# A two-layer graph network on one core: other places for the adjacency's windows, the last tiles' normalisation, and TensorE's branch

## The reference, cut to what matters

```python
# layer 0 (500 hidden features)
h    = sigmoid(h0 @ wenc.T + benc)           # "encoder"
h2   = h @ conv_weight
agg  = segment_sum(h2[src] * edge_weight[:, None], dst)
x    = x + (agg + h @ lin_weight.T) @ wdec.T + bdec
# layer 1
h    = h1 @ W.T + b
deg  = 1 + number of edges with this src
msg  = deg[row]**-0.5 * deg[col]**-0.5 * h[col]     # self loops added
x    = x + segment_sum(msg, row)
```

## Time and profile before

| | us |
|---|---|
| median of 3 runs | 455.64 |
| lowest, highest | 454.35, 456.87 |
| the profiled execution's own time | 455.52 |
| its span | 453.7 |
| TensorE busy in the span | 444.1 |

### The profile page before, as it was taken

How to read it: one execution, slowest core, us unless ns; L and a number is a source line. 1 busy time by engine, 2 the same in 40 slices (tenths; PEclk the granted TensorE clock), 3 DMA queues, 4 the chain that set the end, 5 groups by cost and what they waited for, 6 DMA issues and landing times.

```text
span 453.7 us, 8837 instructions
## 1 busy us (share of the span) xinstructions
PE 444.1 (98%) x3202; PEld 332.8 (73%) x3202; DVE 301.2 (66%) x604; ACT 237.4 (52%) x452; POOL 41.3 (9%) x63
## 2 busy tenths in 40 slices
PE   6999998999999999999999999999999999999997
PEld 4999988978775465469888878888889844444454
DVE  5999895976864243864767776938471657567652
ACT  6987996657769552234244444658463622222220
POOL 2611200000000000000000000464600000000000
PEclk9999999999999999999999999999999999999999
DMA  7950958299457899045800006151758004323433
GB/s 288 306 175 2 173 87 145 70 317 317 143 162 138 265 79 325 3 124 186 302 13 1 1 0 228 53 186 46 287 213 293 1 7 167 129 92 140 156 119 111
DMA packets 48399, 66.37 MB, mean 146 GB/s; under 512 B 25793, under 2 KB 35024, under 8 KB 46820
## 3 DMA queue, kind: packets, MB, share of 16 engines
q1 hardware_dynamic: 48036, 65.39, 48.5%
q0 software_dynamic: 320, 0.39, 0.4%
HBM read 43.62 MB, written 16.77 MB: 133 GB/s over the span
## 4 chain that ended last, share of the span: by engine, by line
PE 84%; ACT 4%; DVE 4%; DMA 4%; SPq 2%; issue 1%; ACTq 0%; DVEq 0%
PE bank L1587 21%; PE bank L1588 21%; PE bank L1589 20%; PE bank L1603 19%; DMA benc_c<-benc 3%; PE bank L1712 2%; DMA h16T<-x 1%; SPq L696 1%; PE bank L1714 1%; ACT h0T L1027 1%; ACT stage L1076 1%; ACT h L979 1%; ACT cnt L1073 1%; DVE stats L1190 1%; DVE h0T L1310 1%
## 5 line engine op out<-in xcount | busy, mean ns | idle before, releaser
L1603 PE MATMUL bank<-a,h_hi 128*128 128x256 f16 (+3 forms) x400 | 85.5, 270 | 0.0
L1603 PE MATMUL bank<-a,h_lo 128*128 128x256 f16 (+3 forms) x400 | 85.5, 270 | 0.0
L1587 PE MATMUL bank<-right,left 128*128 128x512 f16 (+1 forms) x148 | 54.4, 367 | 0.0
L1588 PE MATMUL bank<-right,left 128*128 128x512 f16 (+1 forms) x148 | 54.4, 367 | 0.0
L1589 PE MATMUL bank<-right,left 128*128 128x512 f16 (+1 forms) x148 | 54.4, 367 | 0.0
L1152 ACT CAST left<-zs 128x512 f16<-128x512 f32 x35 | 21.5, 617 | 60.3 <-PE bank L1589 60.3
L1572 DVE SCALAR_TENSOR_TENSOR x<-bank,dis_u,x 128x512 f32<-128x512 f32 (+2 forms) x37 | 26.7, 722 | 34.2 <-PE bank L1589 34.2
L1587 PE MATMUL bank<-h0T,we 128*128 128x256 f32 (+3 forms) x144 | 41.4, 287 | 1.0 <-DVE h0T L1308 1.0
L1603 PEld LDWEIGHTS bank<-a,h_hi 128*128 128x128 f16 (+1 forms) x400 | 38.9, 97 | 4.2 <-issue 0.3
L1603 PEld LDWEIGHTS bank<-a,h_lo 128*128 128x128 f16 (+1 forms) x400 | 39.1, 98 | 3.8
L1587 PE MATMUL bank<-unit,g 128*128 128x500 f16 (+3 forms) x120 | 40.8, 340 | 0.0
(11 more groups left out here) (191 smaller groups left out, 978.2 us busy)
## 6 DMA issues: line engine op xcount, KB each, us to landing
whole<-w SPq DMA_DIRECT2D x7, 1024.0 KB, 7.8
adj_scratch<-stage SPq DMA_DIRECT2D x50, 125.0 KB, 3.5
right_scratch<-right SPq DMA_DIRECT2D x5, 1024.0 KB, 4.0
right<-right_scratch SPq DMA_DIRECT2D x5, 1024.0 KB, 4.8
h<-x SPq DMA_DIRECT2D x9, 512.0 KB, 6.7
x<-x SPq DMA_DIRECT2D x9, 512.0 KB, 5.4
out<-x SPq DMA_DIRECT2D x18, 256.0 KB
w_tile<-w SPq DMA_DIRECT2D x8, 512.0 KB, 4.9
```

Source lines behind the costliest of these rows:

```text
L1587: pe.matmul(o, lhs[0], rhs[0], start=first, stop=False, skip_group_check=True)
L1588: pe.matmul(o, lhs[0], rhs[1], start=False, stop=False, skip_group_check=True)
L1603: ins = pe.matmul(o, h1[i][0:n, k, 128 * f:128 * (f + 1)], moving, start=(k == 0 and part == 0 and i == 0), stop=(k == T - 1 and part == p ...
```

## The change

1. `due` is bent: 22 windows instead of 26 are due beside the encoder. Behind the groups from `("e", 1, 3)` there are now two or one, and 23 windows (0 to 22) stand ahead of `("g", 0)`. Behind `("g", 3)`, `("g", 5)` and `("g", 8)` stand three windows (29 to 31, 34 to 36, 41 to 43), and behind the other `g` and `swl` groups two.
2. ACT's normalisation of tiles 6 to 9 is two steps, `high` (L977) and `norm` (the f32 pass), with other work between them. The abs-sum of the conv weights (`("size", "wc")`, L993) moves from behind `("e", 2, 1)` to behind `("e", 1, 1)`. The turns of tiles 8 and 9 now stand together behind `("e", 2, 3)`; the cuts of the conv weights move from beside block 4 into blocks 3 and 4.
3. The maximum over partitions for the scales goes by one small matmul (`("spread", "wc")`) that broadcasts the 128 sums through the identity into a PSUM bank, and DVE reads that, instead of two DMAs through DRAM. It takes a turn in the rotation of six banks.
4. TensorE's program is written twice behind one test of the flag; the test ahead of layer 1 is gone.
5. The 2 KB load of `benc` is issued behind the second tile of x instead of behind the sixth. One abs-sum and load of `w1` moves from beside `swl` into layer 0's second stage, `bounds` two steps later.

```diff
+SLOW = 22
...
     beside = {
-        (1, 0): turn(2)[:2] + fourth[1:3] + turn(2)[2:], (1, 1): fourth[3:], (1, 2): [("norm", 6)] + fifth[:1], (1, 3): [("norm", 7), ("split", 6), ("turn", 6)],
-        (2, 0): [("split", 7), ("turn", 7)] + fifth[1:], (2, 1): [("size", "wc")], (2, 2): both(turn(3)) + [("norm", 8)],
-        (2, 3): [("norm", 9), ("split", 8), ("turn", 8), ("limits", "out")],
-        (3, 0): [("split", 9), ("turn", 9)], (3, 1): [("limits", "in")], (3, 2): both(turn(4)),
-        (4, 0): [("limits", "scale")], (4, 1): cut_wc[:1], (4, 2): cut_wc[1:3], (4, 3): cut_wc[3:],
+        (1, 0): turn(2)[:2] + fourth[1:3] + turn(2)[2:], (1, 1): fourth[3:] + [("size", "wc")], (1, 2): [("high", 6)] + fifth[:1], (1, 3): [("norm", 6), ("split", 6), ("turn", 6), ("high", 7)],
+        (2, 0): [("norm", 7), ("split", 7), ("turn", 7)] + fifth[1:], (2, 1): [("high", 8)], (2, 2): [("norm", 8)] + both(turn(3)) + [("high", 9)],
+        (2, 3): [("split", 8), ("turn", 8), ("norm", 9), ("split", 9), ("turn", 9), ("spread", "wc")],
+        (3, 0): [("limits", "scale")], (3, 1): cut_wc[:1], (3, 2): both(turn(4)), (3, 3): cut_wc[1:2],
+        (4, 0): cut_wc[2:3], (4, 1): cut_wc[3:],
     }
...
     def due(w):
-        return w + OPEN * (NW - w) / NW
+        if w < SLOW:
+            return OPEN + (share - OPEN) * w / SLOW
+        return share + (NW - share) * (w - SLOW) / (NW - SLOW)
+
+    groups = [s[0] for s in dense[dense.index(("edges",)):] if s[0] in ("e", "g", "swl")]
+    share = NW * groups.count("e") / len(groups)
...
-                elif s == ("limits", "out"):
-                    sp.wait_ge(sizes_ready, 1)
-                    sp.dma_start(limit_row, sizes[:]).then_inc(limits_out, 16)
...
+                elif s[0] == "high":
+                    t = s[1]
+                    n = tile_rows(t)
+                    act.wait_ge(rstd_ready, t // 2 + 1)
+                    if t >= 2 * BY_DMA + 2:
+                        act.wait_ge(turned[t - 2], 32)
...
+                    if s == ("spread", "wc"):
+                        pe.wait_ge(sizes_ready, 1)
+                        pe.matmul(take(s)[:, 0:P], sizes[:].broadcast_to([P, P]), ident[:], start=True, stop=True,
+                                  skip_group_check=True).then_inc(acc_ready, 1)
...
+            m = pe.value_load(missed[0:1, 0:1], min_val=0, max_val=1)
+            with pe.If(m == 0):
+                run(STEPS[general + 1:], (0,))
+            with pe.If(m != 0):
```

More of the change, by code:

```diff
@@ L192, in schedule @@
     dense += [("load", "wl")] + [("g", t) for t in range(4)] + mix(cut_wl, [("g", t) for t in range(4, T)]) + opening[:2]
-    for k, s in enumerate([("g", 2), ("g", 4), ("g", 6), ("g", 8), opening[0]]):
+    for k, s in enumerate([("g", 2), ("g", 4), ("g", 6), ("g", 8)]):
         i = dense.index(s) + 1
@@ L253, in schedule @@
                 steps += [("row", "in"), ("load", "wd")]
-            if n == 1 and k in (1, 2, 3):
-                steps += [("size", "w1", KD - 4 + k)] + [("load", "w1", KD - 2 + k)] * (k == 1)
+            if n == 1 and k in (1, 2, 3, 4):
+                steps += [("size", "w1", KD - 5 + k)] + [("load", "w1", KD - 3 + k)] * (k < 3)
             if n and sums and (n, k) != (1, 0):
@@ L358, in build @@
             frees[s[1:]] = len(frees)
+        elif s == ("limits", "scale"):
+            frees["spread", "wc"] = len(frees)
     nth = {(p, b): p * NB + b for p in range(NP) for b in range(NB)}
@@ L419, in build @@
         minus_half = small("minus_half", [P, 2], F32)
-        sizes = small("sizes", [P, 2], F32)
+        sizes = small("sizes", [P, 1], F32)
         ew_sizes = small("ew_sizes", [EP, 1], F32)
@@ L605, in build @@
         relu_ready = sem("relu_ready")
+        high_ready = sem("high_ready")
         split_ready = sem("split_ready")
@@ L698, in _ @@
                     sp.dma_start(ew_raw[:], nat_w).then_inc(ew_in, 16)
+                    sp.dma_start(benc_c[:], benc).then_inc(benc_in, 16)
                 if t == 3:
@@ L991, in _ @@
                     loaded(act, "wc", 0)
-                    act.wait_ge(size_blank, 1)
-                    nc.scalar.activation(wc_abs[:], wc_raw[:], ACT.Abs, accum_out=sizes[:, 0:1]).then_inc(sizes_ready, 1)
+                    nc.scalar.activation(wc_abs[:], wc_raw[:], ACT.Abs, accum_out=sizes[:]).then_inc(sizes_ready, 1)
                 elif s[0] == "degree":
@@ new lines, in _, with pair, counted @@
+            general = STEPS.index(("general",))
+            run(STEPS[:general], (0,))
+            pe.wait_ge(missed_ready, 1)
+            m = pe.value_load(missed[0:1, 0:1], min_val=0, max_val=1)
+            with pe.If(m == 0):
+                run(STEPS[general + 1:], (0,))
+            with pe.If(m != 0):
+                def pair(k, first):
+                    pe.wait_ge(gen_pair, k + 1)
+                    key, o = gen_key[:], wbank[0]
+                    pe.matmul(o[:, 0:WC], gen_src[0][:], key, start=first, stop=False, skip_group_check=True)
+                    for part in gen_src[1:]:
+                        ins = pe.matmul(o[:, WC:2 * WC], part[:], key, start=False, stop=False, skip_group_check=True)
+                    ins.then_inc(gen_used, 1)
+                def counted(k, first):
+                    pe.wait_ge(gen_pair, k + NW * CH + 1)
+                    pe.matmul(wbank[0][:, 0:WC], gen_src[0][:], gen_key[:], start=first, stop=False,
+                              skip_group_check=True).then_inc(gen_used, 1)
+                pe.wait_ge(stage_ready, NW)
+                with pe.Fori(0, NW) as w:
+                    pe.wait_ge(gen_deg, w + 1)
+                    pair(w * CH, True)
+                    with pe.Fori(1, CH) as c:
+                        pair(w * CH + c, False)
+                pe.wait_ge(gen_stage, 3 * NW)
+                with pe.Fori(0, NW) as w:
+                    counted(w * CH, True)
+                    with pe.Fori(1, CH) as c:
+                        counted(w * CH + c, False)
+                pe.wait_ge(gen_rest, 2 * NW)
+                run(STEPS[general + 1:], (0, 1))
```

326 lines of the change are left out of this document (142 added, 184 removed).

## The result

| | before | changed |
|---|---|---|
| median, us | 455.39 (4 runs) | 460.99 (4 runs) |
| lowest, highest | 454.35, 456.87 | 460.55, 462.53 |
| profiled execution, its span | 455.52, 453.7 | 462.53, 460.6 |

The ratio is 1.0131, 95% interval 1.0114 to 1.0148: slower by 5.6 us. The forecast was 460.7.

A forecast was written before the change was run, and what follows sets the result against it. TensorE, busy in 98% of the span, bounds the kernel, so only its waits matter. Terms 2.0 + 0.7 - 1.1 + 3.6 = +5.2 on 455.52 give 460.7 us, range 457.6 to 463.0.

The forecast's parts named there:

- The normalisation, +2.0: Beside the encoder: ACT waits 4.9 us for POOL's scales at tile 8's high half; block 4 starts 2.0 later.
- rival 3: Beside the encoder: fewer windows relieve ACT, waits of 2.9 us go, 452.6 us; chance 0.07.
- a variance on DVE by 48: Condition of rival 3: scales of tiles 8 and 9 by 51.5 need DVE's var at 48.
- Behind block 4's input, +0.7 and -1.1: Around block 4: two windows that come later cost 0.7; the waits at 78.86 and 92.23 go, -1.1.
- The places of three, +3.6: Third windows at ("g", 3), ("g", 5) and the third place wait 1.0, 1.8 and 0.8; bounds 2.3 and 4.2.
- rival 1: POOL's scales: the short time, ready at 55.3, chain 1.1 earlier, 459.6 us; inside the forecast's 0.82.
- The branch, 0: TensorE's test after the windows keeps its 0.75; dropping the test ahead of layer 1 gains 0; bound -0.75.
- rival 4: After the windows: if the jump over the unwanted body cost, 0.75 goes, 460.0 us; chance 0.3, inside the forecast.
- The scales by a matmul, 0: One small matmul while TensorE waits for block 3, two DMAs off SP's queue: cost 0; without cover 0.2.
- Abs-sum, `benc`, `w1` steps: 0: Abs-sum fits ACT's idle 1.99, 0; earlier `benc` -0.4 to +0.4, taken 0; `w1` steps in layer 0, 0, up to 0.5.

The follow-up runs named there:

- run 1: The changed kernel again with no edit, against the kernel before: 461.19 us against 454.65, ratio 1.014.
- run 3: The changed kernel with the variance of tiles 8 and 9 ahead of tile 6's split on DVE: 457.17 us, ratio 1.0067 to the kernel before.
- run 2: The changed kernel with the old rule for due windows, no place of three: 457.58 us, ratio 1.006 to the kernel before.
- run 8: The kernel before with the bent rule for due windows alone: 458.81 us, ratio 1.0085.
- run 6: The changed kernel with DVE making window matrices three windows ahead instead of two: 460.05 us, ratio 1.0124 to the kernel before.
- run 7: The changed kernel with TensorE's program written once behind the test and the second test ahead of layer 1 back: 461.19 us.
- run 10: The changed kernel with old window rule, early variance, and the maximum by two DMAs behind tile 9's turns: 463.42 us, ratio 1.0199 to the kernel before.
- run 12: The kernel before with the small matmul for the maximum instead of the two DMAs, alone: 455.29 us, ratio 1.0004.
- run 9: The changed kernel with old window rule, early variance and matrices three windows ahead: 453.18 us, ratio 0.997 to the kernel before.
- run 11: The changed kernel with tile 8's high half behind the copies for block 3 on ACT: 461.24 us, ratio 1.0144 to the kernel before.
- the two faster versions: The changed kernel with old window rule and early variance, 453.81 us; the same with matrices three windows ahead, 453.18 us.

## Why the prediction was right, term by term

**The normalisation, +2.0: right in its mechanism and to 0.1.** ACT's wait was placed at 51.5 to 56.4, 4.9; it was 51.53 to 56.19, 4.66. Block 3 was put at 61.7 and started at 61.51; block 4 at 77.2 and started at 77.08. There is some luck in the 77.08: the waits that I placed before windows 9 and 11 are in run 1's trace, but in this one 1.3 of low clock stood in their place. The 2.0 was only the difference to a kernel that itself had waits there; freed of the wait, the same order gains 4.0 (run 3). By the prediction's terms it would be 4.5: the 2.0 and 0.7 go, and rival 3's relief is 2.9 where I had 1.1. What is missing is about what still waits before windows 9 and 11 in run 3, 0.41 and 0.25 of idle time. Its condition, a variance on DVE by 48, was the right one: with it at 45.74 the wait was gone. One row I hadn't foreseen, 0.63 before window 6 for DVE's matrices, lies ahead of the wait for block 3 and adds nothing.

**Behind block 4's input, +0.7 and -1.1: right in the trace.** No wait answers to 78.86 or 92.23.

**The places of three, +3.6: right, with one releaser wrong.** 1.03, 1.90 and 0.87 from start to start, 3.8, against 1.0, 1.8 and 0.8; taken out, 3.6 (run 2, where the windows go back beside the encoder), and on the kernel before 4.2 (run 8). At the third place I named ACT; it is DVE, whose matrices stand behind a cut of `wl` and a low part there too. Its price was near the bank's price (0.8 in run 6), so the sum did not notice.

**POOL's time, rival 1.** 3.1 from 53.06 to 56.16, near the 3.4 that I took. Run 3 put the same chain beside other work, and there the row speaks more plainly. POOL and DVE in its trace:

```profile
45.98 1.72 POOL L895 TENSOR_TENSOR std<-dis,minus_half 128x2 f32<-128x2 f32 x1 [5.41 <-DVE dis L1230]
```
```profile
45.91 1.23 DVE L1295 TENSOR_TENSOR x<-h,x 128x1024 f16<-128x1024 f32 x1
```

POOL's first instruction took 1.72 instead of 0.71 and 0.81, while DVE ran a split with two inputs in SBUF until 47.14; beside DVE's copies of 38.08, of which one input is a PSUM bank, the whole chain took 2.2. By the rule quoted in the prediction from the Trainium skill, SBUF — State Buffer, section "SBUF: two separate sides", this is what it should do; these rows agree.

**The branch, 0, and rival 4.** The 0.75 became 0.50, and is 0.75 again with the old form (run 7). I had given all or nothing; it is a third, and below what the time shows. Which part of the form makes it, the fall-through or something else, was not taken apart.

**The scales by a matmul, 0: wrong as a reason, harmless in the sum.** I looked at TensorE's 0.2 and at two DMAs off SP's queue, and did not ask what those DMAs do to what stands behind them. The stage buffers' DMAs behind the first of them took 5.3 to 5.7 instead of 2.2, and ACT waited 1.56 for one of them ahead of block 4's copies (run 10). For the turns I took the median of 4.7 in the earlier trace rows, but they vary from 3.2 to 5.3 in that trace; in the changed kernel the median is 3.3. Without the DMAs the input of block 4 is there 2.7 earlier (run 12), 0.4 of which that whole trace is ahead. In the changed kernel that gain is hidden, since there TensorE reached block 4 only at 77.08. In run 9's version it should count, since block 4 starts at 74.04 there; and run 10, where the DMAs are back, lost 9.6.

**Abs-sum, `benc`, `w1` steps: 0.** ACT's wait for `benc` is gone (its first sigmoid starts at 21.05 with none) and nothing is later by more than the starts of these kernels differ among themselves; no row behind 140 us has a wait. None of them was run alone.

**The sum.** 5.2 forecast, 5.6 and 6.5 measured in the two comparisons. By the trace: 1.9 and 0.7 at block 4, less 1.1, 3.8 at the places of three, less 0.25: 5.05; the profiled execution adds the 1.6 of the second stretch of low clock, 6.65 of the 6.9 by which the spans differ. Run 1's trace, at the full clock, gives the same: its waits up to 139 us are 8.6 from start to start, those of the kernel before 3.6. What the medians of run 1 show over that 5 is 1.5. For 0.9 of it the traced execution of the kernel before lies above its median there (455.52 against 454.65); the rest has no single wait behind it and stays open.

## What to carry to other kernels

When a step is moved ahead on one engine, follow its input back to the instruction that makes it, and move that too: here the high half went ahead by 6 us and the variance that it needs stayed, and all that was queued behind it paid. A slot shared by more pieces of work than it has buffers costs a wait at each place, however well the totals balance: here two windows behind a group are free, and the third costs 0.8 at least. And a wait removed by moving the waiting instruction comes back on the next one when the engine is loaded behind it (run 11).

## What the runs showed of the hardware

- A DMA of 4 bytes from each of 128 partitions to DRAM took 8.2 us to land, and held up 125 KB DMAs issued behind it on the same queue to 11.1; with 8 bytes a partition, at another place in the queue, 5.6 and 5.6 (4.7 and 4.8 in run 8). Without it they take 2.2 in the same stretch. Transposing DMAs of 128x1024 f16 took 3.2 to 5.3, and which of them are slow is not explained by it.
- Long waits of TensorE can be followed by a granted clock of 0.50 for some microseconds, in some executions and not in others: behind the same waits of 1.29 and 1.74 it is 0.50 in the first profile and 1.00 in run 1's. By the mean clock of whole executions, none of 56 executions of the kernel before, and none of 20 of the two faster versions, had a mean clock under 0.992; of the five of run 6, whose window 7 waits 1.80, two had, of the six of run 11 with the wait of 2.46 three, and of the five of run 10 with the wait of 6.62 all; of the nine of the changed kernel one had, and of the six of run 3 one. The mean is a rough measure: run 11's profiled execution has 0.996 and yet 5 us at 0.66. Which waits are followed by it, and why not each time, is open.
- Seven small POOL instructions on 128x2 took 2.2 to 3.7 us from the first start to the last end, by what DVE ran beside them.
